# Latent attention of a two-layer kernel: four score banks, row maxima as single full-depth products, and no bank of their own for sums and outputs

## The chip, the cores and the metric

One core of one Trainium2 chip runs the whole program. The metric is the device time of one execution in microseconds, lower is better; the time of the kernel is the median of several executions.

## The reference, cut to what matters

The program is two transformer layers; the change lies in the first layer's attention alone. Per batch (B = 16) there are S = 100 queries in H = 16 heads and 1444 keys. The keys and the values are one and the same latent of 64 numbers, shared by all heads.

```
q_big = rope(einsum('bshk,hkq->bshq', (x @ Wq.T).reshape(B, S, H, K), w_kc_q))
kv_r  = rope(ctx)                                  # (B, 1444, 64)
q_r   = einsum('bshq,hqr->bhsr', q_big, W_qr)
k_r   = einsum('bld,hdr->bhlr', kv_r, W_kr)
attn  = softmax(einsum('bhsr,bhlr->bhsl', q_r, k_r), axis=-1)
ctx_c = einsum('bhsl,bld->bhsd', attn, kv_r)       # then w_kc_kv, Wo, + x
```

Before this stage the weights are folded, so that per batch there remains a query of 64 numbers for each of 1600 rows (head, position), which meets the 1444 latents directly. Queries and keys are held as a high part (fp32r) and the rest, for accuracy.

## The kernel before

**Stage and tiling.** `latent_attention` runs 16 batches in software pipeline. A batch has two halves p of eight heads and 12 tiles of 128 keys (`KT`), so `NS` = 24 values n = p * 12 + t; the program walks them in pairs, m = n // 2, from 0 to 11. Each n has two score tiles (o = 0, 1), 128 keys by 400 columns (four heads by 100 queries). Four score tiles belong to an m. Each engine has its order written out by hand in its own `step`, and semaphores (`at_...`) join the engines; nothing reorders them.

**A score tile.** `scores` (L814) makes it of two matmuls, KH x QS and KB x QB, into bank `S0 + (2n+o) % SB`, here three banks. KH holds the high part of the keys twice (rows 0 to 63 and 64 to 127), QS the high part of the queries and their rest, and the KB, QB pair the remaining product and the row maximum, which is subtracted inside the matmul. ScalarE (L780) takes the exponential into one of eight buffers of R. `values` (L824) multiplies R with KV, two n at a time and one m late, into bank CTX, in two halves of 64 columns of the array. VectorE (`sum_even`, L606 to L612) adds the tiles of o = 0 up in bank ACC, GpSimd (`sum_odd`, L628) those of o = 1 in EA.

**The row maxima.** The softmax maxima of batch b + 1 are found during batch b. `NF` = 39 products (13 tiles of 128 queries by 3 pieces of 482 keys) are made in 20 pairs: `max_pair` (L567) issues two matmuls of 64 rows, which use the upper and the lower half of the array at the same time, into banks F0 and F0 + 1, and one `reduce_pair` (L590) on VectorE reduces both banks to two columns of PM. Pair i waits for the reduction of pair i - 1. Two pairs stand in each of m = 0 to 9. `batch_max` (L596) then makes NM, `turn_max` (L573) transposes it, ScalarE and VectorE split it into MH and ML, and two DMAs bring these into QB, for which the next batch's first score waits.

**Sums and output.** `sums` (L637) reduces the accumulated exponentials over the partitions by a matmul with ones, for the earlier batch's second half at m = 2 (`SUM_AT`) and this batch's first half at m = 8 (`SUM0_AT`); `sums_out` on ScalarE copies them, a chain over `reciprocals` (L653, in n = 9) and DMAs leads to `divide` (L659, in n = 14), and `project` (L666) at m = 9 makes the earlier batch's output, which `add_output` adds. Sums, transpose and output share bank MISC. Banks: scores 0 to 2, maxima 3 and 4, CTX 5, ACC 6, MISC 7.

**Beside it.** GpSimd, ScalarE and VectorE also prepare the keys of batch b + 2 (`rotate_part`, `keys_high`); VectorE's part (L540, the lower part KB) comes at n = 18 and n = 20. The first batch has no earlier one beside it: its 20 pairs stand alone, in four banks, `max_pair` two deep. The last batch makes no maxima.

Of the kernel before, what the change touches and what calls it, by code (L numbers as in the profile page):

```python
# [20 lines left out]
P = 128  # L21
# [56 lines left out]
def as_f32(ap):  # L78

    return ap.bitcast(F32)  # L80
# [312 lines left out]
def latent_attention(core, dram, X, ident, queries, recips, BB):  # L393
# [25 lines left out]
    with ExitStack() as ctx:  # L419
# [127 lines left out]

        def f_bank(b, i):

            return S0 if b is FIRST and i % 2 else F0  # L550

        def pieces(i):
            return range(2 * i, min(2 * i + 2, NF))

        def max_pair(pe, b, i):

            r = b_mod(b)
            depth = 2 if b is FIRST else 1
            if i >= depth:
                pe.wait_ge(red_done, b_val(b) * NP + (i - depth + 1))  # L560
            elif b is not FIRST:
                pe.wait_ge(red_done, b_val(b) * NP)
            for f in pieces(i):
                t, j = divmod(f, KC)
                rows = slice((f % 2) * DC, (f % 2 + 1) * DC)
                high = QB if f % 2 else QS
                last = nc.tensor.matmul(psum[f_bank(b, i) + f % 2][:, 0:KW], high[r][rows, t * P:(t + 1) * P],  # L567
                                        KH[r][rows, KAT[j]:KAT[j] + KW], start=True, stop=True)
            last.then_inc(f_ready, 1)

        def turn_max(pe, b):
            pe.wait_ge(nm_ready, b_val(b) + 1)
            nc.tensor.transpose(psum[MISC][0:QT, 0:P], NM[:, :], ident[:, :]).then_inc(turned, 1)  # L573

        def max_high(act, b):
            act.wait_ge(turned, b_val(b) + 1)
            if b is not FIRST:
                act.wait_ge(m_in, b_val(b) * 32)
            nc.scalar.activation(MH[:, :], psum[MISC][0:QT, 0:P], ACT.Copy).then_inc(mh_ready, 1)

        def max_low(v, b):
            v.wait_ge(mh_ready, b_val(b) + 1)
            nc.vector.tensor_tensor(ML[:, :], psum[MISC][0:QT, 0:P], as_f32(MH[:, :]), ALU.subtract).then_inc(ml_ready, 1)

        def reduce_pair(v, b, i):
            v.wait_ge(f_ready, b_val(b) * NP + (i + 1))
            if i == 0 and b is not FIRST:
                v.wait_ge(nm_ready, b_val(b))
            k, n = f_bank(b, i), len(pieces(i))
            nc.vector.tensor_reduce(PM[:, 2 * i:2 * i + n], banks[:, k:k + n, 0:KW], AX.X, ALU.max).then_inc(red_done, 1)  # L590

        def batch_max(v, b):
            v.wait_ge(red_done, b_val(b) * NP + NP)
# [36 lines left out]
        def sums(pe, b, p):  # L630

            pe.wait_ge(even_sum, b_val(b) * NS + (EB + KT * (p + 1)))
            pe.wait_ge(odd_sum, b_val(b) * 2 * ADDS + ADDS * (p + 1))
            if p == 0 and b is not FIRST:
                pe.wait_ge(su_done, b_val(b) * 2)
            for o in range(2):
                last = nc.tensor.matmul(psum[MISC][o * DC:(o + 1) * DC, 0:CH], ones[:], ES[:, p, o, :], start=True, stop=True)  # L637
            last.then_inc(sum_done, 1)

        def sums_out(act, b, p):  # L640
            act.wait_ge(sum_done, b_val(b) * 2 + (p + 1))
            if b is not FIRST:
                act.wait_ge(sr_in, b_val(b) * 32)
            nc.scalar.activation(SU[:, p, :], psum[MISC][0:DC + 1, 0:CH], ACT.Copy).then_inc(su_done, 1)

# [16 lines left out]
        def project(pe, b):  # L662

            pe.wait_ge(ct_ready, b_val(b) + 2)
            for j in range(H // 2):
                last = nc.tensor.matmul(psum[MISC][0:S, 0:D], CT[:, j, :], BB[:, j, :], start=j == 0, stop=j == H // 2 - 1)  # L666
            last.then_inc(out_ready, 1)

        def add_output(v, b):
            v.wait_ge(out_ready, b_val(b) + 2)  # L670
            x = X[:, b_val(b), :]
            nc.vector.tensor_tensor(x, psum[MISC][0:S, 0:D], x, ALU.add).then_inc(res_done, 1)

# [11 lines left out]
        def b_mod(b):  # L685
            return b.r
# [14 lines left out]
        with nc.Block() as block:  # L701
# [50 lines left out]
            def _(act):  # L752
# [13 lines left out]
                def step(b, has_next, has_keys):  # L766
                    for n in range(NS):
                        if n == 2 * TURN_AT + 2 and has_next:
                            max_high(act, b + 1)
                        if n == 0 and b is not FIRST:  # L770
                            context_out(act, before(b), 1)
                        act.wait_ge(av_done, b_val(b) * NS + (n + 1))
                        act.wait_ge(even_sum, b_val(b) * NS + (n + 1))
# [7 lines left out]
                        if n in HI_AT and has_keys:  # L781
                            keys_high(act, b + 2, HI_AT.index(n))
                        if n == 2 * SUM_AT + 1 and b is not FIRST:
                            sums_out(act, before(b), 1)
                        if n == KT + 1:
                            context_out(act, b, 0)
                        if n == 2 * SUM0_AT + 1:
                            sums_out(act, b, 0)

# [5 lines left out]
            def _(pe):  # L795
# [5 lines left out]
                for i in range(NP):  # L801
                    max_pair(pe, FIRST, i)
                turn_max(pe, FIRST)
# [23 lines left out]

                def step(b, has_next, has_keys):
                    for m in range(NS // 2):
# [12 lines left out]
                        for n in (2 * m, 2 * m + 1):  # L842
                            scores(b, n)
                        if has_next and m and 2 * m + 1 < NP:
                            max_pair(pe, b + 1, 2 * m + 1)
                        if m == TURN_AT and has_next:
                            pe.wait_ge(su_done, b_val(b) * 2 + 1)
                            if b is not FIRST:
                                pe.wait_ge(res_done, b_val(b))
                            turn_max(pe, b + 1)  # L850
# [3 lines left out]
                        if m == SUM_AT and b is not FIRST:  # L854
                            sums(pe, before(b), 1)
                        if m == SUM0_AT:
                            sums(pe, b, 0)
                        if m == OUT_AT and b is not FIRST:
                            pe.wait_ge(su_done, b_val(b) * 2 + 1)
                            project(pe, before(b))  # L860

                steps(pe, step)
                for n in range(NS - 2, NS):
                    values(LAST, n)
                pe.wait_ge(res_done, B - 1)
                sums(pe, LAST, 1)
                pe.wait_ge(su_done, 2 * B)
                project(pe, LAST)

            @block.vector  # L870
            def _(v):
# [21 lines left out]
                for i in range(NP):  # L893
                    reduce_pair(v, FIRST, i)
                batch_max(v, FIRST)
# [4 lines left out]
                def step(b, has_next, has_keys):  # L900
                    for n in range(NS):
                        if has_next and n < NP:
                            reduce_pair(v, b + 1, n)
# [4 lines left out]
                        if has_next and n == NP - 1:  # L908
                            batch_max(v, b + 1)
# [4 lines left out]
                        if n == CT_AT and b is not FIRST:  # L914
                            divide(v, before(b))
                        if n == 2 * OUT_AT + 2 and b is not FIRST:
                            add_output(v, before(b))
                        if n == 2 * TURN_AT + 2 and has_next:
                            max_low(v, b + 1)

                steps(v, step)
# [1502 lines left out]
```

## Time and profile before

| | |
|---|---|
| median of 3 runs | 1990.33 us (1978.36 to 1990.39) |
| profiled execution, its own time | 1987.93 us |
| span of the profile | 1986.1 us |
| latent attention, first to last maximum product, then its tail | 309.7 to 1131, to 1207 us |
| TensorE matmul busy | 1710.8 us (86%) |
| VectorE, GpSimd, ScalarE busy | 1313.9, 902.8, 769.1 us |

The profile is one execution. PE is TensorE's matmuls and PEld its weight loads, which may overlap matmuls; DVE is VectorE, ACT ScalarE, POOL GpSimd, SP the engine that issues DMAs. A matmul's row lasts from its start to the modelled arrival of its last result, so neighbours overlap in time, and the time that each costs the stream is the distance from start to start. The rows below are read that way.

### The profile page before, as it was taken

The numbers are of one execution on the slowest core, as the hardware profiler recorded it, in microseconds if no ns is written. First come the engines' busy times: TensorE is split into PE (matmuls) and PEld (weight loads), VectorE is DVE, ScalarE is ACT, GpSimd is POOL, SyncE is SP. The second block draws the span as 40 slices with busy tenths as digits, with TensorE's granted clock in tenths as the row PEclk, the third lists the DMA queues.
The fourth block names the chain that finished last, engine by engine and source line by source line (L and its number), as shares of the span: only waits on it lengthen the run. The fifth ranks groups of instructions, "written<-read, shape, count | busy, mean of one in ns | idle before, by whom it ended". The sixth has DMA issues, their size and how long they took to land. (4 is left out here: it accounts for less than half of the span.)

```text
span 1986.1 us, 29082 instructions
## 1 busy us (share of the span) xinstructions
PE 1710.8 (86%) x9602; PEld 1155.4 (58%) x9602; DVE 1313.9 (66%) x2408; ACT 769.1 (39%) x1996; POOL 902.8 (45%) x800
## 2 busy tenths in 40 slices
PE   4999935999999999999999996499999559987890
PEld 3677712555555555555555553399999547664780
DVE  5577768777777777777777744377767666666333
ACT  2100001444444444444444442266656237652230
POOL 0366623777777777777777440223322100000436
PEclk9999965999999999999999996599999879988795
DMA  6133344122122221122221002545555250001243
GB/s 183 39 72 71 67 125 150 39 72 61 45 72 72 72 64 56 63 72 72 72 72 35 10 9 54 152 163 201 183 173 196 85 130 0 0 1 37 89 122 102
DMA packets 91670, 166.50 MB, mean 84 GB/s; under 512 B 45635, under 2 KB 70439, under 8 KB 86735
## 3 DMA queue, kind: packets, MB, share of 16 engines
q1 hardware_dynamic: 83727, 145.77, 23.8%
q0 software_dynamic: 7808, 19.02, 3.8%
q8 instruction: 73, 1.20, 0.3%
q14 instruction: 62, 0.51, 0.1%
HBM read 134.91 MB, written 29.53 MB: 83 GB/s over the span
## 5 line engine op out<-in xcount | busy, mean ns | idle before, releaser
L780 ACT ACTIVATE R<-banks 128x400 f32<-128x400 f32 x768 | 333.7, 505 | 342.4 <-PE banks L814 340.0
L590 DVE TENSOR_REDUCE PM<-banks 128x2 f32<-128x964 f32 x320 | 360.8, 1132 | 155.8 <-PE banks L567 154.1
L628 POOL TENSOR_TENSOR EA<-EA,R 128x400 f32<-128x400 f32 x288 | 313.3, 1088 | 177.8 <-ACT R L780 164.6
L814 PE MATMUL banks<-QS,KH 128*128 128x400 f32 x768 | 309.5, 403 | 3.0 <-DMA QB<-ML 2.1
L824 PE MATMUL banks<-R,KV 128*64 128x400 f32 x1536 | 299.9, 512 | 0.0
L814 PE MATMUL banks<-QB,KB 128*128 128x400 f32 x768 | 266.2, 347 | 0.0
L608 DVE TENSOR_TENSOR banks<-banks,R 128x400 f32<-128x400 f32 x320 | 183.9, 575 | 54.9 <-ACT R L780 54.2
L814 PEld LDWEIGHTS banks<-QS,KH 128*128 128x128 f32 x768 | 145.2, 189 | 109.0 <-ACT R L780 58.5
L567 PE MATMUL banks<-KH,QS 64*128 64x482 f32 x320 | 160.5, 502 | 53.5 <-DVE KB L540 46.3
L175 PE MATMUL banks<-e_xh,e_split 128*116 128x256 f32 x960 | 195.7, 287 | 4.0 <-DVE e_xl L1586 4.0
L380 POOL TENSOR_TENSOR rotated<-rope_prod 96x400 f32<-96x400 f32 x128 | 131.7, 1049 | 131.7 <-DVE rope_prod L357 131.6
L567 PEld LDWEIGHTS banks<-KH,QS 64*128 64x128 f32 x320 | 60.9, 191 | 197.2 <-issue 111.6
L824 PEld LDWEIGHTS banks<-R,KV 128*64 128x64 f32 x1536 | 93.4, 136 | 120.0 <-ACT R L780 67.1
L357 DVE TENSOR_TENSOR rope_prod<-banks,rope_q 96x400 f32<-96x400 f32 x256 | 128.6, 561 | 51.0 <-PE banks L175 51.0
L175 PEld LDWEIGHTS banks<-e_xh,e_split 128*116 128x116 f32 x960 | 153.1, 183 | 4.4 <-DVE e_xl L1586 4.4
L567 PE MATMUL banks<-KH,QB 64*128 64x482 f32 x304 | 153.0, 504 | 0.0
L814 PEld LDWEIGHTS banks<-QB,KB 128*128 128x128 f32 x768 | 146.5, 191 | 0.4
L1461 POOL DMA_INDIRECT results<-e_ys,m_target x40 | 44.4, 1109 | 213.1 <-DVE e_ys L1604 207.0
L175 PE MATMUL banks<-e_xl,e_split 128*116 128x256 f32 x480 | 136.7, 285 | 0.0
L521 POOL TENSOR_TENSOR raw<-raw,ropeT 128x722 f32<-128x722 f32 x60 | 104.0, 1735 | 53.8 <-DMA rawk<-in_ctx_k 53.8
L1052 POOL IOTA m_steps<- 100x7 f32 (+1 forms) x2 | 0.3, 158 | 237.8 <-POOLq L70 237.8
L1611 DVE TENSOR_TENSOR e_HF<-banks,e_G 116x256 f32<-116x256 f32 x120 | 50.5, 421 | 86.9 <-ACT e_G L1550 85.9
(281 smaller groups left out, 3368.9 us busy)
## 6 DMA issues: line engine op xcount, KB each, us to landing
m_stage_u<-in_m_up SPq DMA_DIRECT2D x20, 1392.0 KB
raw<-in_ctx_T SPq DMA_DIRECT2D x16, 1444.0 KB, 6.2
m_stage_d<-in_m_down SPq DMA_DIRECT2D x20, 696.0 KB
QS<-queries SPq DMA_DIRECT2D x16, 800.0 KB, 6.8
queries<-q_out_h SPq DMA_DIRECT2D x64, 100.0 KB, 2.4
queries<-q_out_l SPq DMA_DIRECT2D x64, 100.0 KB, 2.4
QB<-queries SPq DMA_DIRECT2D x16, 400.0 KB, 8.1
RS<-recips SPq DMA_DIRECT2D x32, 200.0 KB
```

Source lines behind the costliest of these rows:

```text
L175: ins = nc.tensor.matmul(out, lhs, rhs, start=first and n == 0, stop=last and n == len(todo) - 1)
L357: last = nc.vector.tensor_tensor(prod[:, h % 2, n, :].rearrange("p (b s) -> p b s", b=CB), psum[2 * (h % 2) + half][0:HALF, 0:CH].rearrang ...
L380: last = nc.gpsimd.tensor_tensor(rot[:, h % TURNS, half, :], prod[:, h % 2, 2 * half, :], prod[:, h % 2, 2 * half + 1, :], ALU.add)
L521: ins = ops.tensor_tensor(raw[:, row, half], raw[:, row, half], ropeT[:, row, half], ALU.mult)
L567: last = nc.tensor.matmul(psum[f_bank(b, i) + f % 2][:, 0:KW], high[r][rows, t * P:(t + 1) * P], KH[r][rows, KAT[j]:KAT[j] + KW], start=Tr ...
L590: nc.vector.tensor_reduce(PM[:, 2 * i:2 * i + n], banks[:, k:k + n, 0:KW], AX.X, ALU.max).then_inc(red_done, 1)
L608: ins = nc.vector.tensor_tensor(acc, acc, tile_of(n, 0), ALU.add)
L628: nc.gpsimd.tensor_tensor(out, first, tile_of(n, 1), ALU.add).then_inc(odd_sum, 1)
L780: nc.scalar.activation(tile_of(n, o), psum[S0 + (2 * n + o) % SB][:, 0:CH], ACT.Exp).then_inc(exp_done, 1)
L814: last = nc.tensor.matmul(out, lhs[r][:, keys], heads[:, o], start=lhs is KH, stop=lhs is KB)
L824: last = nc.tensor.matmul(psum[CTX][o * DC:(o + 1) * DC, 0:CH], KV[b_mod(b)][:, t, :], tile_of(n, o), start=t == 0, stop=t == KT - 1)
L1611: nc.vector.tensor_tensor(HF[:, b, :], psum[b][0:TR, TOK:2 * TOK], G[:, b, :], ALU.mult).then_inc(h_ready, 1)
```

## The change

- **Banks.** Scores get four banks (0 to 3, `SB` = 4), the maxima banks 4 and 5, CTX 6, ACC 7. MISC is gone: sums, transpose and its readers use the first bank of the maxima (F0), the output projection the second (F0 + 1).
- **Maxima.** `max_row` (L560 in the changed file) issues one product over all 128 rows, KH x QS, to bank F0 + f % 2, and waits for reduction f - 2; `reduce_row` (L610) reduces one bank. The table `MAX_AT` gives each m up to four slots: before the scores, between the two n, after them, and after the values. The first batch's maxima are still reduced in pairs (`first_max`, `first_reduce`), of full-depth products.
- **Guards.** Since banks are shared, `max_row` at f = 12 and f = 34 waits for ScalarE's copy of the sums, f = 0 and 1 for ML and the added output, `sums` for the reduction of the bank's last product.
- **Order.** The transpose now follows the values of m = 10, and the output projection moves from m = 9 to right behind it; `add_output` moves from n = 20 to n = 22; `batch_max` from n = 19 to n = 20.

```diff
-    SB, FB = 3, 2
+    SB = 4
-    S0, F0, CTX, ACC, MISC = 0, 3, 5, 6, 7
-    SUM_AT, SUM0_AT, OUT_AT, TURN_AT = 2, 8, 9, 10
+    S0, F0, CTX, ACC = 0, 4, 6, 7
+    SUM_AT, SUM0_AT, TURN_AT = 2, 8, 10
+    MAX_AT = ((1, 1, 1, 1),) * 3 + ((0, 1, 1, 1),) + ((1, 1, 1, 1),) * 4 + ((1, 1, 1, 0), (0, 1, 1, 1), (1, 1, 0, 0), (0, 0, 0, 0))
+    MAX_NO = [[sum(map(sum, MAX_AT[:m])) + sum(MAX_AT[m][:slot]) for slot in range(4)] for m in range(NS // 2)]
+    MAX_SUM, MAX_SUM0 = MAX_NO[SUM_AT + 1][0], MAX_NO[SUM0_AT + 1][0]
...
+        def max_product(b, f, bank):
+            t, j = divmod(f, KC)
+            return nc.tensor.matmul(psum[bank][:, 0:KW], QS[b_mod(b)][:, t * P:(t + 1) * P],
+                                    KH[b_mod(b)][:, KAT[j]:KAT[j] + KW], start=True, stop=True)
...
+        def max_row(pe, b, f):
+            if f == 0:
+                pe.wait_ge(ml_ready, b_val(b))
+            elif f == 1:
+                if b_val(b) >= 3:
+                    pe.wait_ge(res_done, b_val(b) - 2)
+            else:
+                pe.wait_ge(red_done, max_base(b) + (f - 1))
+            if f == MAX_SUM and b_val(b) >= 2:
+                pe.wait_ge(su_done, 2 * b_val(b) - 2)
+            if f == MAX_SUM0:
+                pe.wait_ge(su_done, 2 * b_val(b) - 1)
+            max_product(b, f, F0 + f % 2).then_inc(f_ready, 1)
...
+        def reduce_row(v, b, f):
+            v.wait_ge(f_ready, max_base(b) + (f + 1))
+            if f == 0:
                 v.wait_ge(nm_ready, b_val(b))
-            k, n = f_bank(b, i), len(pieces(i))
-            nc.vector.tensor_reduce(PM[:, 2 * i:2 * i + n], banks[:, k:k + n, 0:KW], AX.X, ALU.max).then_inc(red_done, 1)
+            nc.vector.tensor_reduce(PM[:, f:f + 1], psum[F0 + f % 2][:, 0:KW], AX.X, ALU.max).then_inc(red_done, 1)
...
                     for m in range(NS // 2):
...
-                        if has_next and 2 * m < NP:
-                            max_pair(pe, b + 1, 2 * m)
+                        max_slot(m, 0)
                         if m == 0:
                             if b is not FIRST:
                                 for n in range(NS - 2, NS):
                                     values(before(b), n)
-                            if has_next:
-                                max_pair(pe, b + 1, 1)
                             pe.wait_ge(m_in, b_val(b) * 32 + 32)
-                        for n in (2 * m, 2 * m + 1):
-                            scores(b, n)
-                        if has_next and m and 2 * m + 1 < NP:
-                            max_pair(pe, b + 1, 2 * m + 1)
-                        if m == TURN_AT and has_next:
...
+                        scores(b, 2 * m)
+                        max_slot(m, 1)
+                        scores(b, 2 * m + 1)
+                        max_slot(m, 2)
                         for n in (2 * m - 2, 2 * m - 1):
                             if n >= 0:
                                 values(b, n)
...
+                        max_slot(m, 3)
+                        if m == TURN_AT:
+                            if has_next:
+                                turn_max(pe, b + 1)
...
+                            if b is not FIRST:
+                                project(pe, before(b))
```

What this does to the order, at two places. In the names, KH0, QS0, QB0 and KB0 belong to the batch whose maxima are made, KH2, QS2, QB2 and KB2 to the batch whose scores are made. First TensorE at the end of m = 0 and the start of m = 1, before:

```order
L567 MATMUL banks<-KH0,QS0 128x482 [waits at_red]
L567 MATMUL banks<-KH0,QB0 128x482
L814 MATMUL banks<-QS2,KH2 128x400 [waits at_exp,at_min]
L814 MATMUL banks<-QB2,KB2 128x400
...
L814 MATMUL banks<-QS2,KH2 128x400 [waits at_exp]
L814 MATMUL banks<-QB2,KB2 128x400
L567 MATMUL banks<-KH0,QS0 128x482 [waits at_red]
L567 MATMUL banks<-KH0,QB0 128x482
L814 MATMUL banks<-QS2,KH2 128x400 [waits at_exp]
```

and in the changed kernel:

```order
L834 MATMUL banks<-QB2,KB2 128x400
L560 MATMUL banks<-KH0,QS0 128x482 [waits at_res]
L834 MATMUL banks<-QS2,KH2 128x400 [waits at_exp]
L834 MATMUL banks<-QB2,KB2 128x400
L834 MATMUL banks<-QS2,KH2 128x400 [waits at_exp]
L834 MATMUL banks<-QB2,KB2 128x400
L560 MATMUL banks<-KH0,QS0 128x482 [waits at_red] x3
L834 MATMUL banks<-QS2,KH2 128x400 [waits at_exp]
```

A pair stood after four score tiles; now product f = 1 stands after two of them, and f = 2, 3 and 4 stand in a row, each waiting for the reduction two places back. Second, VectorE in n = 18 and 19 (m = 9), before:

```order
L608 TENSOR_TENSOR banks<-banks,R 128x400 [waits at_evensum,at_exp]
L540 TENSOR_TENSOR KB0<-raw,KH0 64x722 [waits at_kh,at_rotstep]
L590 TENSOR_REDUCE PM<-banks 128x1 [waits at_f]
L608 TENSOR_TENSOR banks<-banks,R 128x400 [waits at_evensum,at_exp]
L596 TENSOR_REDUCE NM<-PM 128x13 [waits at_turned,at_red]
```

and in the changed kernel, from n = 18 to n = 20:

```order
L610 TENSOR_REDUCE PM<-banks 128x1 [waits at_f]
L544 TENSOR_TENSOR KB0<-raw,KH0 64x722 [waits at_kh,at_rotstep]
L610 TENSOR_REDUCE PM<-banks 128x1 [waits at_f]
L628 TENSOR_TENSOR banks<-banks,R 128x400 [waits at_evensum,at_exp]
L610 TENSOR_REDUCE PM<-banks 128x1 [waits at_f] x2
L628 TENSOR_TENSOR banks<-banks,R 128x400 [waits at_evensum,at_exp]
L610 TENSOR_REDUCE PM<-banks 128x1 [waits at_f]
L616 TENSOR_REDUCE NM<-PM 128x13 [waits at_turned,at_red]
```

Behind the first half of KB only one reduction was left; now four are, of the products f = 35 to 38.

## Rows read from the trace of the kernel before

**Rows 1.** Busy time of every engine in stretches (us, PE, PEld, DVE, ACT, POOL, then PEclk, DMA)

```profile
660.19:713.80 53.61, 53.61 (x260) 28.80 (x258) 39.78 (x51) 24.25 (x55) 39.17 (x33) 1.00 0.21 67
...
300.00:330.00 30.00, 14.40 (x39) 5.57 (x39) 28.87 (x31) 1.50 (x2) 12.27 (x9) 0.50 0.46 145
```

**Rows 2.** Timeline of PE, one m: start us, length us, engine, line, operation

```profile
681.85 0.48 PE L567 MATMUL banks<-KH,QS 64*128 64x482 f32 x1
...
682.27 0.45 PE L814 MATMUL banks<-QS,KH 128*128 128x400 f32 x1
682.56 0.34 PE L814 MATMUL banks<-QB,KB 128*128 128x400 f32 x1
...
683.29 0.34 PE L814 MATMUL banks<-QB,KB 128*128 128x400 f32 x1
683.58 0.46 PE L814 MATMUL banks<-QS,KH 128*128 128x400 f32 x1
683.88 0.34 PE L814 MATMUL banks<-QB,KB 128*128 128x400 f32 x1
684.15 0.48 PE L567 MATMUL banks<-KH,QS 64*128 64x482 f32 x1
...
684.57 1.56 PE L824 MATMUL banks<-R,KV 128*64 128x400 f32 x8
686.06 0.48 PE L567 MATMUL banks<-KH,QS 64*128 64x482 f32 x1
```

**Rows 3.** Timeline of PE, scores straight after values

```profile
656.83 0.45 PE L814 MATMUL banks<-QS,KH 128*128 128x400 f32 x1
657.12 0.34 PE L814 MATMUL banks<-QB,KB 128*128 128x400 f32 x1
```

**Rows 4.** PE weight loads: timeline, then the list of waits for 350 to 1200 us

```profile
683.58 0.19 PEld L814 LDWEIGHTS banks<-QS,KH 128*128 128x128 f32 x1 [0.28 <-ACT R L780]
...
PEld banks L814 <- ACT R L780: 56.7, 202, 0.6
```

**Rows 5.** Timeline of ACT

```profile
683.02 1.74 ACT L780 ACTIVATE R<-banks 128x400 f32<-128x400 f32 x4 [2.47 <-PE banks L814]
```

**Rows 6.** Groups by form (count, busy us, mean ns); line 540 (ns min/median/max)

```profile
L590 DVE TENSOR_REDUCE PM<-banks 128x2 f32<-128x964 f32 x304 | 350.3, 1157 | 154.8 <-PE banks L567 153.5
...
L590 DVE TENSOR_REDUCE PM<-banks 128x1 f32<-128x482 f32 x16 | 10.5, 658 | 1.1 <-PE banks L567 0.6
...
L540 DVE TENSOR_TENSOR KB<-raw,KH x32: 903/909/1745, 307.8 to 1080.7; 64x722 fp32r<-64x722 f32 x32
```

**Rows 7.** Timelines of DVE (the last row: of POOL)

```profile
681.55 0.57 DVE L608 TENSOR_TENSOR banks<-banks,R 128x400 f32<-128x400 f32 x1
682.03 0.75 DVE L653 RECIPROCAL RR<-SR 16x100 f32<-16x100 f32 x1
...
684.68 1.16 DVE L590 TENSOR_REDUCE PM<-banks 128x2 f32<-128x964 f32 x1 [0.39 <-PE banks L567]
...
692.35 0.98 DVE L659 TENSOR_TENSOR CT<-CU,RS 128x800 f32<-128x800 f32 x1
...
701.55 1.75 DVE L540 TENSOR_TENSOR KB<-raw,KH 64x722 fp32r<-64x722 f32 x1
703.32 0.66 DVE L590 TENSOR_REDUCE PM<-banks 128x1 f32<-128x482 f32 x1
704.01 0.58 DVE L608 TENSOR_TENSOR banks<-banks,R 128x400 f32<-128x400 f32 x1
...
1131.39 0.66 DVE L590 TENSOR_REDUCE PM<-banks 128x1 f32<-128x482 f32 x1 [0.62 <-PE banks L567]
1131.96 0.57 DVE L608 TENSOR_TENSOR banks<-banks,R 128x400 f32<-128x400 f32 x1
...
701.48 1.04 POOL L628 TENSOR_TENSOR EA<-EA,R 128x400 f32<-128x400 f32 x1 [2.11 <-ACT R L780]
```

**Rows 8.** The first batch: timeline of DVE

```profile
310.47 20.96 DVE L590 TENSOR_REDUCE PM<-banks 128x2 f32<-128x964 f32 x20 [0.95 <-PE banks L567]
```

More of the change, by code:

```diff
@@ L411, in latent_attention @@
     PAD = -1.0e30
-    S0, F0, CTX, ACC, MISC = 0, 3, 5, 6, 7
-    SUM_AT, SUM0_AT, OUT_AT, TURN_AT = 2, 8, 9, 10
+    S0, F0, CTX, ACC = 0, 4, 6, 7
[3 more added lines that the diff above has]
+    MAX_SUM, MAX_SUM0 = MAX_NO[SUM_AT + 1][0], MAX_NO[SUM0_AT + 1][0]
+    assert sum(map(sum, MAX_AT)) == NF and MAX_SUM % 2 == 0 and MAX_SUM0 % 2 == 0
     RECIP_AT, CT_AT = 9, 14
@@ L546, in keys_high, with max_base @@
             nc.scalar.activation(KH[b_mod(b)][:, half], raw[:, 0, half], ACT.Copy).then_inc(kh_ready, 1)
-        def f_bank(b, i):
-            return S0 if b is FIRST and i % 2 else F0
+        def max_base(b):
+            return NP + (b_val(b) - 1) * NF if b is not FIRST else 0
         def pieces(i):
             return range(2 * i, min(2 * i + 2, NF))
[L555 to L562, printed above, removed]
-            for f in pieces(i):
[L564 to L568, printed above, removed]
-            last.then_inc(f_ready, 1)
+        def max_product(b, f, bank):
+            t, j = divmod(f, KC)
+            return nc.tensor.matmul(psum[bank][:, 0:KW], QS[b_mod(b)][:, t * P:(t + 1) * P],
+                                    KH[b_mod(b)][:, KAT[j]:KAT[j] + KW], start=True, stop=True)
@@ L636, in sums @@
             for o in range(2):
-                last = nc.tensor.matmul(psum[MISC][o * DC:(o + 1) * DC, 0:CH], ones[:], ES[:, p, o, :], start=True, stop=True)
+                last = nc.tensor.matmul(psum[F0][o * DC:(o + 1) * DC, 0:CH], ones[:], ES[:, p, o, :], start=True, stop=True)
             last.then_inc(sum_done, 1)
@@ L665, in project @@
             for j in range(H // 2):
-                last = nc.tensor.matmul(psum[MISC][0:S, 0:D], CT[:, j, :], BB[:, j, :], start=j == 0, stop=j == H // 2 - 1)
+                last = nc.tensor.matmul(psum[F0 + 1][0:S, 0:D], CT[:, j, :], BB[:, j, :], start=j == 0, stop=j == H // 2 - 1)
             last.then_inc(out_ready, 1)
@@ L771, in step @@
                             context_out(act, before(b), 1)
+                        if n == 2 * SUM_AT + 2 and b is not FIRST:
+                            sums_out(act, before(b), 1)
+                        if n == 2 * SUM0_AT + 2:
+                            sums_out(act, b, 0)
                         act.wait_ge(av_done, b_val(b) * NS + (n + 1))
@@ L801, in _ @@
                 for i in range(NP):
-                    max_pair(pe, FIRST, i)
+                    first_max(pe, i)
                 turn_max(pe, FIRST)
@@ L828, in step, with max_slot @@
                 def step(b, has_next, has_keys):
+                    def max_slot(m, slot):
+                        if has_next and MAX_AT[m][slot]:
+                            max_row(pe, b + 1, MAX_NO[m][slot])
                     for m in range(NS // 2):
@@ L854, in step @@
                         if m == SUM_AT and b is not FIRST:
+                            if has_next:
+                                pe.wait_ge(red_done, max_base(b + 1) + (MAX_SUM - 1))
+                            else:
+                                pe.wait_ge(ml_ready, b_val(b) + 1)
                             sums(pe, before(b), 1)
                         if m == SUM0_AT:
+                            if has_next:
+                                pe.wait_ge(red_done, max_base(b + 1) + (MAX_SUM0 - 1))
                             sums(pe, b, 0)
-                        if m == OUT_AT and b is not FIRST:
-                            pe.wait_ge(su_done, b_val(b) * 2 + 1)
-                            project(pe, before(b))
+                        max_slot(m, 3)
+                        if m == TURN_AT:
+                            if has_next:
+                                turn_max(pe, b + 1)
+                            elif b is not FIRST:
+                                pe.wait_ge(res_done, b_val(b) - 1)
+                            if b is not FIRST:
+                                project(pe, before(b))
                 steps(pe, step)
@@ L915, in step @@
                             divide(v, before(b))
-                        if n == 2 * OUT_AT + 2 and b is not FIRST:
-                            add_output(v, before(b))
                         if n == 2 * TURN_AT + 2 and has_next:
                             max_low(v, b + 1)
+                        if n == 2 * TURN_AT + 2 and b is not FIRST:
+                            add_output(v, before(b))
                 steps(v, step)
```

46 lines of the change are left out of this document (23 added, 23 removed).

## The prediction

> **What bounds the kernel now.** I went from the coarse view to the fine one. The window over one whole batch of the latent attention [rows 1] shows TensorE busy for all of 53.61 us at the full clock (1.00, 2.4 GHz), VectorE for 39.78, ScalarE for 24.25, GpSimd for 39.17. So TensorE's own stream is the batch: a term counts only if it lengthens or shortens that stream. "Busy" hides small losses, though, because a matmul's row lasts longer than its turn. I therefore read start to start [rows 2], over m = 5: a pair of 64-row maximum products 0.42 us (681.85 to 682.27), eight score products 1.88 (to 684.15), a second pair 0.42, the values 1.49 (684.57 to 686.06). That is 4.21 us, and it repeats. Inside the 1.88 the normal step is 0.183 us (four from 682.56 to 683.29), but the first takes 0.29 (0.11 more; the same after values [rows 3]), the last, ahead of 64-row products, 0.27 (0.10 more, counting both roundings), and the two from 683.29 to 683.88 take 0.59. There the weight load stood until 683.58 for an exponential [rows 4]: ScalarE began the first of that m at 683.02 and needs 0.5 us (four take 1.74 in steps of 0.41) [rows 5]. With three score banks the fourth tile needs the bank of the first. The list of waits counts 202 such waits, once for nearly each of the 16 x 12 values of m.
>
> **What the fourth bank removes.** Eight normal steps are 1.46; with the 0.11 and the 0.10 they make 1.67, and 0.21 us of the 1.88 are the wait. With four banks a tile needs the exponential four tiles back, which by then has had about 2.5 us of maxima and values to finish in. ScalarE has four at about 0.41 us each per 4.2 us, so nothing takes this wait's place there. I take all of it: 12 x 0.21 = **-2.5 us per batch**.
>
> **The maximum products.** Before: 19 pairs at 0.415 and one single at 0.41, 8.3 us. After: 39 products of the full depth, 482 columns. No row shows one. Its nearest row is the score product, 400 columns in 0.183 us; in proportion it is 0.22, and 482 columns at 2.4 GHz are 0.20. I take 0.217, 8.5 us: **+0.2 us** (bounds -0.5 and +0.3). They have the scores' tile shape, so between scores they need no extra 0.11. The blocks between values stay 12 (the lone product between the two blocks of values at m = 0 costs 0.21, the merged maxima of m = 0 and 1 save 0.21), and scores at m = 10 are now followed by values instead of the transpose: **+0.1**. Sums, transpose and output projection change place but not length; ScalarE's copies of the sums keep their place between exponentials, and the chain recips, RS, divide had no wait at its divide in a middle batch. The transpose now comes after values and before the projection, so its 3.35 us still lie ahead of the next batch's scores, as cover for the max row's DMAs.
>
> **The reductions.** One reduction of 964 elements took 1.157 us, one of 482 took 0.658 [rows 6]; 39 of these are 25.7 us against 22.6, so VectorE gets 3.1 us more per batch, 43 of 53.6. As a sum that is hidden: an m then costs it four steps of 0.57 (1131.39 to 1131.96) and two even sums of 0.48 (681.55 to 682.03) [rows 7], 3.25 us of about 4.0. What binds is latency: two banks now serve as a ring of single products, and product f waits for reduction f-2. Before, a pair waited for a reduction that had 1.9 us or more.
>
> **The new waits, worked out.** A pair's reduction starts 0.53 us after its first product (684.15 to 684.68) [rows 2, 7], 0.05 after the product's row of 0.48 ends. A full product in the stream has a row of about 0.38 (a score's 0.34, 82 columns more), so its reduction starts 0.43 after it; the first in a block, 0.54. Then 0.658, and 0.05 for the signal (exponential's end at 683.53, load at 683.58) [rows 4, 5]. A full product that was held pays 0.11 for its uncovered load. (a) f = 2, 3, 4 stand in a row, since m = 0 has no values of its own batch: f = 4 would follow f = 2 by two steps of 0.22 and the 0.08 that f = 3 waits, 0.51 us, but may start its work only 0.43 + 0.66 + 0.05 + 0.11 = 1.25 after it: 0.73. f = 3 and 5 lose 0.08 and 0.11, by the same steps. (b) In the usual m the second product has, from the product behind the values, 0.33 + 0.22 + 0.73 = 1.28 of cover, and needs 0.54 + 0.66 + 0.05 + 0.11 = 1.36: 0.08, five times, 0.4. (c) The reciprocal (0.75) [rows 7] now comes ahead of the reduction of the next m's first product: 0.3. (d) The divide (0.98) in m = 7: 0.15. (e) In m = 9 the half of KB (701.55, 1.75 us) stands between the reductions of f = 34 and 35: f = 37 may start at 0.43 + 0.58 + 1.77 + 0.66 + 0.05 + 0.11 = 3.60 after f = 34, and the stream brings it at 3.09: 0.5, and f = 38 another 0.1. Together **+2.4 us per batch** at 14 or 15 batches. (e) depends on GpSimd: the 1.75 us row began while GpSimd was busy from 701.48 [rows 7], while the middle one of the 32 such operations took 0.91 [rows 6]. The Trainium skill (SBUF — State Buffer, Who interferes with whom) says that a VectorE operation with two SBUF inputs and a GpSimd one that reads SBUF exclude each other by a lock; this trace agrees, 1.75 us against 0.91. If by shifted timing the lock is missed, (e) goes, 0.5 us per batch or 8 in all; I keep it, since the GpSimd sum stands at the same tile in both kernels.
>
> **Outside the steady batches.** The last batch has no maxima and keeps its whole gain, -2.5. In the first batch's 39 products, the clock is at 1.2 GHz (0.50 in [rows 1]) and VectorE's reductions set the pace: twenty in 20.96 us, the last a single, 1.07 each [rows 8]. Serial full products take 0.40 each there instead of two at once: signal 0.05, load 0.17, first 0.40, second to its reduction 0.66, and 1.16 of reduction make 2.44 per two pairs against 2.14: 0.15 x 19 = +2.8, if the clock stays at 1.2; 0 if it rises.
>
> **Sum.** 15 x (-2.5 + 0.2 + 0.1 + 2.4) = 15 x 0.2 = +3.0; -2.5; +2.8: +3 us on the profiled execution's 1987.93, which is 1991. The three runs' median is 1990.33, 2.4 above it, so **1991 us** stands for the median as well. The wait for the exponential is replaced by one for the reductions of nearly the same size.
>
> **Rivals.** (1) *The ring holds less than I count.* If reductions start sooner after a product (0.35) and follow one another at 0.50, the waits fall to about 1.2 us per batch: 15 x (-2.2 + 1.2) - 2.5 + 2.8 = -15, 1973. With no waits it is 15 x -2.2 + 0.3 = -33: 1955. For it: VectorE is idle 14 us of a batch. Against: (a) and (e) follow from the order alone. (2) *VectorE's pace is worse, slower.* The one single reduction in a middle batch held VectorE for 0.69 (703.32 to 704.01) [rows 7], not 0.57. At 0.69 an m costs 3.7 us, and (b) to (e) grow from 1.5 to 2.6: 15 x 1.2 + 0.3 = +18, 2006; if each reduction also starts 0.54 after its product and not 0.43, +2.0 per batch, 2018. It decides from +1.3 us per batch on, a pace of about 0.7. [...] Against: the row follows the KB operation, and 1131.39 without it has 0.57. (3) *The fourth bank does nothing*, because the wait at 683.58 is for something else that stays: then 15 x 2.7 + 2.8 = +43: 2031. Against: it ends 0.05 after the exponential's end.
>
> **How the numbers follow.** Forecast (within 12 us of 1991) 0.60; (1) 0.21; (2) 0.16; (3) 0.03. The ends of the forecast are -0.5 and +0.3 on the products, 0.5 on (e), 3 at the start. The range reaches halfway into (1) and over most of (2): 1966 to 2011. A measurement tells 1%, 20 us, from no change: faster (under 1970) is most of (1), 0.16; slower (over 2010) is the worse part of (2) and (3), 0.12; same 0.72.
>
> **What would show it.** In the profile after: the score tiles' load waits on ScalarE gone, eight scores and four products in a row 0.18 and 0.22 apart; weight loads of the maximum products waiting on the reductions, the longest at f = 4 and f = 37, with a sum near 2.4 us per batch (36 in all); a batch of 53.6 to 53.9 us; reductions near 0.66. I am wrong if the full products step above 0.25, if the waits on reductions sum to under 1.4 or over 3.5 us per batch, or if the exponentials still hold scores.

## The result, and the profile after

The changed kernel takes **2009.93 us** (median of 4 runs, 2004.01 to 2015.11) against 1988.63 for the kernel before (4 runs): ratio 1.0124, interval 1.0086 to 1.0161. It is slower by 1.2%; the forecast was no change, 1991 us. The profiled execution took 2004.01 us, 16.1 more than the 1987.93 of before; it is the shortest of the four.

The page's first lines and the costliest groups of the changed kernel (engine, busy us, share, count; then line, busy us, mean ns, idle before) answer to [rows 6]:

```profile
PE 1702.0 (85%) x9602; PEld 1217.0 (61%) x9602; DVE 1338.0 (67%) x2693; ACT 780.5 (39%) x1996; POOL 908.4 (45%) x800
...
L610 DVE TENSOR_REDUCE PM<-banks 128x1 f32<-128x482 f32 x585 | 365.0, 650 | 161.7 <-PE banks L560 161.1
...
L560 PE MATMUL banks<-KH,QS 128*128 128x482 f32 x624 | 262.1, 452 | 71.7 <-DVE KB L544 46.2
```

TensorE is busy for 9 us less in a span 16 us longer: the loss is idle time. The list of waits from 350 to 1220 us says on whom (us, times, longest) and answers to [rows 4]:

```profile
PEld banks L560 <- DVE PM L610: 58.5, 118, 3.4
...
PEld banks L834 <- DMA QB<-ML: 8.5, 6, 3.6
...
PEld banks L834 <- ACT R L804: 0.6, 1, 0.6
```

The waits of scores on ScalarE are gone but for one of 0.6 us; they were 56.7 us in 202 before. Those on reductions were to be 36 us, the longest under 1 us; they are 58.5, the longest 3.4.

**Where in time.** A fixed landmark is the reciprocal, once per batch. From the first to the 14th of these there are 697.4 us before (413.94 to 1111.30, twelve periods of 53.61 to 53.63 and a last one of 53.91) and 716.4 after (415.75 to 1132.11): +19.0. Of 13 periods after, eight are 54.06 to 54.15; the others are 55.79, 56.81, 58.25, 58.25 and 54.41. So 13 x 0.47 = 6 us are lost evenly and 13 us in five batches. At the first reciprocal the changed kernel is 1.8 us late, and from the 14th to the last it gives back 3.5. One ordinary batch in windows (columns as in [rows 1]), whose first row there it answers to; the second answers to the other, and the third follows it:

```profile
757.00:811.10 54.10, 53.02 (x257) 32.51 (x256) 40.90 (x71) 25.05 (x55) 39.72 (x33) 1.00 0.21 67
300.00:330.00 30.00, 17.25 (x32) 8.15 (x32) 26.99 (x29) 1.50 (x2) 10.82 (x8) 0.50 0.47 145
340.00:350.00 10.00, 9.54 (x37) 6.87 (x36) 6.43 (x12) 4.77 (x9) 4.15 (x4) 0.80 0.90 310
```

**The ring's waits are as forecast.** PE's timeline at the three products in a row (f = 2 to 5; scores of L834 between), then at f = 37:

```profile
671.28 0.35 PE L834 MATMUL banks<-QB,KB 128*128 128x400 f32 x1
671.47 0.35 PE L834 MATMUL banks<-QS,KH 128*128 128x400 f32 x1
671.65 0.35 PE L834 MATMUL banks<-QB,KB 128*128 128x400 f32 x1
671.84 0.65 PE L560 MATMUL banks<-KH,QS 128*128 128x482 f32 x2
672.98 0.49 PE L560 MATMUL banks<-KH,QS 128*128 128x482 f32 x1 [0.49 <-DVE PM L610]
673.30 0.35 PE L834 MATMUL banks<-QS,KH 128*128 128x400 f32 x1
...
657.01 0.49 PE L560 MATMUL banks<-KH,QS 128*128 128x482 f32 x1
657.72 0.48 PE L560 MATMUL banks<-KH,QS 128*128 128x482 f32 x1 [0.21 <-DVE PM L610]
```

f = 4 starts 1.14 us after f = 2, where two free steps are 0.44: 0.70 lost, forecast 0.81 (0.73 and the 0.08 of f = 3). At 657.72 the step is 0.71 and not 0.22: 0.5, forecast 0.5. Scores step 0.185, undisturbed by exponentials.

**The divide is not.** Its line, as minimum, median and maximum ns, in the changed kernel:

```profile
L679 DVE TENSOR_TENSOR CT<-CU,RS x16: 991/1634/4380, 425.8 to 1216.4; 128x800 f32<-128x800 f32 x16
```

In [rows 7] it took 0.98 us. Two batches of the changed kernel, VectorE and GpSimd, the ordinary case first:

```profile
646.01 0.65 DVE L610 TENSOR_REDUCE PM<-banks 128x1 f32<-128x482 f32 x1
646.58 1.65 DVE L679 TENSOR_TENSOR CT<-CU,RS 128x800 f32<-128x800 f32 x1
...
646.35 1.03 POOL L648 TENSOR_TENSOR EA<-EA,R 128x400 f32<-128x400 f32 x1
647.35 2.57 POOL L539 TENSOR_TENSOR KV<-rawk,prodk 128x768 f32<-128x768 f32 x1
...
700.70 4.34 DVE L679 TENSOR_TENSOR CT<-CU,RS 128x800 f32<-128x800 f32 x1
704.97 0.65 DVE L610 TENSOR_REDUCE PM<-banks 128x1 f32<-128x482 f32 x1
...
700.39 1.05 POOL L648 TENSOR_TENSOR EA<-EA,R 128x400 f32<-128x400 f32 x1
701.39 1.83 POOL L539 TENSOR_TENSOR KV<-rawk,prodk 128x768 f32<-128x768 f32 x1
703.16 1.04 POOL L648 TENSOR_TENSOR EA<-EA,R 128x400 f32<-128x400 f32 x1
```

GpSimd begins a running sum 0.2 to 0.3 us ahead of the divide. In the ordinary case the divide ends 0.85 after that sum's end (647.38), and KV, next on GpSimd, is the one that is stretched: 2.57 against 1.83. At 700.70 KV and the following sum keep their usual length, and the divide ends 0.84 after the end of the *third* GpSimd operation. In the kernel before the divide came first in each of the first 14 batches:

```profile
692.40 1.82 POOL L628 TENSOR_TENSOR EA<-EA,R 128x400 f32<-128x400 f32 x1 [0.18 <-ACT R L780]
```

GpSimd had waited for an exponential there, and the divide of 692.35 slipped in 0.05 us ahead of it; the sum took 1.82 instead of 1.04, which nobody waited for. So the two operations exclude each other. The Trainium skill (SBUF — State Buffer, Who interferes with whom) says the same of VectorE operations with two SBUF inputs and GpSimd operations that read SBUF: an exclusive lock on a shared port pair. By that rule, the trace agrees.

What TensorE made of the 4.34 us (timeline of weight loads, then windows in the columns of [rows 1]):

```profile
705.67 0.19 PEld L560 LDWEIGHTS banks<-KH,QS 128*128 128x128 f32 x1 [3.40 <-DVE PM L610]
```

```profile
702.50:705.50 3.00, 0.07 (x1) 0.00 (x0) 3.00 (x2) 0.00 (x0) 1.70 (x2) 1.00 0.00 0
705.50:710.00 4.50, 4.33 (x15) 3.58 (x17) 3.24 (x7) 2.16 (x5) 1.10 (x2) 0.62 0.00 0
710.00:714.00 4.00, 4.00 (x24) 2.40 (x22) 2.37 (x5) 2.60 (x6) 1.55 (x2) 1.00 0.01 2
```

The maximum product's load stood for 3.4 us behind the reduction queued after the divide. TensorE had done nothing for 3.1 us, and the granted clock fell from 2.4 to 1.2 GHz for a stretch: 0.62 as the mean of the second window, scores 0.33 us apart until about 709, and 1.00 again from 710. In the batch of 589.77, whose load stood just as long (594.73), the loads that follow still take 0.19 us, so the clock had not fallen, and its period is 2.7 us too long, not 4.1: 2.7 is the stall, 1.4 the clock. Three divides of 4.34 to 4.38 cost 11.0 of the 13 uneven us. Most of the rest, 1.7 us of one period, is a load at 505.01 that waited 2.37 us for ML:

```profile
505.01 0.19 PEld L834 LDWEIGHTS banks<-QS,KH 128*128 128x128 f32 x1 [2.37 <-DMA QB<-ML]
```

### The profile page after: what moved, and what is told of

It is laid out like the page before. It is cut to its first block and busy times, and to the rows that moved or that the text cites. A ratio compares the mean times of both kernels' runs of the same rounds, so it can differ in the third digit from the quotient of the medians.

```text
span 2002.2 us, 29381 instructions
## 1 busy us (share of the span) xinstructions
PE 1702.0 (85%) x9602; PEld 1217.0 (61%) x9602; DVE 1338.0 (67%) x2693; ACT 780.5 (39%) x1996; POOL 908.4 (45%) x800
## 5 line engine op out<-in xcount | busy, mean ns | idle before, releaser
L804 ACT ACTIVATE R<-banks 128x400 f32<-128x400 f32 x768 | 342.8, 503 | 346.3 <-PE banks L834 328.6
L610 DVE TENSOR_REDUCE PM<-banks 128x1 f32<-128x482 f32 x585 | 365.0, 650 | 161.7 <-PE banks L560 161.1
L560 PE MATMUL banks<-KH,QS 128*128 128x482 f32 x624 | 262.1, 452 | 71.7 <-DVE KB L544 46.2
L834 PE MATMUL banks<-QS,KH 128*128 128x400 f32 x768 | 275.1, 358 | 4.6 <-DMA QB<-ML 4.6
L834 PE MATMUL banks<-QB,KB 128*128 128x400 f32 x768 | 267.5, 348 | 0.0
L560 PEld LDWEIGHTS banks<-KH,QS 128*128 128x128 f32 x624 | 115.0, 197 | 207.6 <-issue 119.5
L834 PEld LDWEIGHTS banks<-QS,KH 128*128 128x128 f32 x768 | 146.5, 191 | 32.8 <-issue 20.0
L834 PEld LDWEIGHTS banks<-QB,KB 128*128 128x128 f32 x768 | 146.4, 191 | 9.8
L2209 ACT ACTIVATE c_PR<-banks,c_nmax 100x100 f32<-100x100 f32 x256 | 84.2, 356 | 49.6 <-DVE c_nmax L2253 49.6
```

What stands on the lines that cost most here:

```text
L560: return nc.tensor.matmul(psum[bank][:, 0:KW], QS[b_mod(b)][:, t * P:(t + 1) * P], KH[b_mod(b)][:, KAT[j]:KAT[j] + KW], start=True, stop=True)
L610: nc.vector.tensor_reduce(PM[:, f:f + 1], psum[F0 + f % 2][:, 0:KW], AX.X, ALU.max).then_inc(red_done, 1)
L804: nc.scalar.activation(tile_of(n, o), psum[S0 + (2 * n + o) % SB][:, 0:CH], ACT.Exp).then_inc(exp_done, 1)
L834: last = nc.tensor.matmul(out, lhs[r][:, keys], heads[:, o], start=lhs is KH, stop=lhs is KB)
L2209: nc.scalar.activation(PR[u][:, h, :], psum[SC + 2 * u + h // HB][0:S, (h % HB) * S:(h % HB + 1) * S], ACT.Exp, bias=nmax[u][:, 1, h:h + 1 ...
```

## The experiments

Times are medians; "before" is the kernel before on the same chip. A batch is the usual period in steady state, 53.62 before and 54.10 in the changed kernel.

**e1_div_late**: the divide two tiles later, n = 16.

```diff
-    RECIP_AT, CT_AT = 9, 14
+    RECIP_AT, CT_AT = 9, 16
```

> The changed kernel with one number changed: the divide of the earlier batch stands on VectorE in n = 16 and not in n = 14, behind GpSimd's last key-preparation step. Theory A (GpSimd keeps VectorE's divide from starting, 1.6 us in most batches and 4.3 in three of the profile's, 3.4 us of TensorE's stream each plus a stretch at the lower clock): every divide takes 0.98 us, no weight load waits over 1 us for a reduction in mid batch, and the time falls by 10 to 20 us against the changed kernel's 2010, to 1990 to 2000. Theory B (the loss is in the ring of two banks alone, the long divides are a symptom): the time stays within 5 us of 2010.

Measured: 1980.12 against 1985.81, ratio 0.9961 (0.9946 to 0.9977); batch 53.43. One number turns a loss of 1.2% into a gain of 0.4%; the time is 10 us below the expected 1990 to 2000. The divide and the waits on reductions:

```profile
L679 DVE TENSOR_TENSOR CT<-CU,RS x16: 993/1478/1773, 428.1 to 1193.9; 128x800 f32<-128x800 f32 x16
```

```profile
PEld banks L560 <- DVE PM L610: 37.9, 88, 0.8
```

The expected 0.98 did not come: the divide still takes 1.48 us, for GpSimd is busy there too, but never more than 1.8. m = 8 leaves out a product, so little waits for it: where it took 1.77 and not 1.49, the period was 53.48 and not 53.43. The ring with what is left of the divide now waits 37.9 us; the forecast was 36.

**e2_before_div12**: in the kernel before, the divide at n = 12, where GpSimd goes from one operation to the next.

```diff
-    RECIP_AT, CT_AT = 9, 14
+    RECIP_AT, CT_AT = 9, 12
```

> The kernel before with one number changed: the divide stands in n = 12 and not in n = 14, where GpSimd has instructions back to back (668.7 to 692.2 us in the profile of before) and not a pause. Theory A (lock-out by GpSimd, whatever the maxima look like): the divide takes 2 to 4.5 us in most batches, TensorE waits for the pair reductions behind it, and the kernel is slower by 15 to 45 us, 2005 to 2035. Theory B (the long divides belong to the changed kernel's ring): the divide stays at 0.98 us and the time at 1990.

Measured: 2004.85 against 1985.81, 1.0100 (1.0083 to 1.0117); batch 54.84. That is just under the expected 2005 to 2035, and one divide of the 13 took over 2 us, not most of them. One batch:

```profile
697.28 1.98 DVE L659 TENSOR_TENSOR CT<-CU,RS 128x800 f32<-128x800 f32 x1
...
696.68 1.74 POOL L532 TENSOR_TENSOR raw<-raw 128x722 f32<-128x722 f32 x1
698.37 1.79 POOL L628 TENSOR_TENSOR EA<-R 128x400 f32<-128x400 f32 x1
...
700.40 0.18 PEld L567 LDWEIGHTS banks<-KH,QS 64*128 64x128 f32 x1 [1.85 <-DVE PM L590]
```

Nothing of 4 us appears (maximum 2.16): the divide never waited for more than one GpSimd operation, and in every batch it ended 0.85 us after that one.

```profile
643.43 1.00 DVE L659 TENSOR_TENSOR CT<-CU,RS 128x800 f32<-128x800 f32 x1 [1.13 <-DMA RS<-recips]
```

The run is not clean, though. At n = 12 the divide also comes too early for the DMA of RS. Over the 13 batches VectorE stood idle 7 us for that DMA, and the divides were 8 us longer than 0.98 in all; where RS came latest (643.43) the divide took 1.00, and the period was 54.84 as elsewhere. So e2 shows that the exclusion also strikes in the old structure, with its paired reductions, and not that it alone costs 1% there.

**e3_sb3**: the changed kernel with three score banks.

```diff
-    SB = 4
+    SB = 3
```

> The changed kernel with three score banks in use and not four (the fourth serves only the first batch's maxima). My forecast's term: the wait for the exponential comes back, 0.21 us in each of 12 m of 16 batches, less where a wait for a reduction already covers it: slower than the changed kernel by 25 to 40 us, 2035 to 2050. Rival (the fourth bank does nothing): 2010.

Measured: 2027.02 against 1985.81, 1.0200 (1.0180 to 1.0221). Neither 2035 to 2050 nor 2010 came. Beside the changed kernel's 2009.93 it looks as if the bank were worth 17 us, but the profile (2040.25, the longest of the five executions) has eight divides of 4.31 to 4.66 us where the changed kernel's has three, and an ordinary batch is 54.27, only 0.17 more. The time says nothing on the bank; that takes a run without the lock-outs (e10).

**e4_short_reduce**: the reductions read 241 of the 482 columns. This leaves half of the keys out of the maxima.

```diff
-            nc.vector.tensor_reduce(PM[:, f:f + 1], psum[F0 + f % 2][:, 0:KW], AX.X, ALU.max).then_inc(red_done, 1)
+            nc.vector.tensor_reduce(PM[:, f:f + 1], psum[F0 + f % 2][:, 0:KW // 2], AX.X, ALU.max).then_inc(red_done, 1)
```

> The changed kernel in which each single reduction reads 241 of its 482 columns (it leaves out half of the keys' maxima), 0.41 us in place of 0.66. If the ring of two banks costs what I worked out, the waits of about 2.4 us per batch fall to about 0.9, since every one of them holds one reduction's length or more: 15 x 1.5 = 22 us, and VectorE's spare time rises by 9 us a batch. Divides locked out remain, with less behind them. 1975 to 1990. If the ring costs little, within 8 us of 2010.

Measured: 1967.14 against 1985.81, 0.9906 (0.9882 to 0.9929), single runs 1956.33 to 1986.35; batch 51.75. A batch is 2.35 us shorter, and the time is 8 us below what was expected: latency of reductions is what TensorE pays for, though 0.67 of the 2.35 is the divide's (e12). The wide spread probably goes with the divide: in this profile two take 5.57 us, behind four GpSimd operations in a row, and the four runs of e12 lie within 4.1 us.

**e9_before_div16**: control, the kernel before with the divide at n = 16 (diff as in e1).

> Control: the kernel before with the divide in n = 16, the same edit that took 30 us off the changed kernel. In the kernel before, the divide of n = 14 already took 0.98 us, in a pause of GpSimd, so there is nothing to win: within 5 us of the kernel before (about 1986). If it gains 10 us or more, the edit has another effect than the one I name, and the 30 us are not all lock-out.

Measured: 1984.30 against 1987.90, 0.9991 (0.9972 to 1.0010); divide 0.98, batch 53.61. The move alone brings nothing; what e1 won is the repair of a loss that the change had made.

**e10_sb3_div16**: the changed kernel with `CT_AT` = 16 and `SB` = 3.

> The changed kernel with the divide in n = 16 and three score banks. The run with three banks and the divide in n = 14 had a batch of 54.3 us against 54.1 with four, so my theory is that the fourth bank is worth 0.2 us a batch: 3 to 5 us slower than the run with four banks and the divide in n = 16 (1980), 1983 to 1986. The maximum product between the second and the third score tile gives ScalarE the 0.2 us that the fourth tile used to wait. My forecast's term (2.5 us a batch from the bank itself) would give 2018.

Measured: 1981.57 against 1987.90, 0.9968 (0.9951 to 0.9986); batch 53.60 against 53.43 in e1. In a batch with maxima the fourth bank is worth **0.17 us**; the times of e10 and e1 lie within each other's intervals. The wait of [rows 4] is nearly gone without it:

```profile
PEld banks L834 <- ACT R L804: 7.8, 28, 0.3
...
711.58 0.19 PEld L834 LDWEIGHTS banks<-QS,KH 128*128 128x128 f32 x1 [0.28 <-ACT R L804]
```

Where the 28 stand tells why. In a batch with maxima it is one (in one batch two), at m = 11 (the row), the one m that has no maximum product between its score pairs. In the last batch, without maxima, it is again one for nearly each m (12 from 1142 us on), and there the bank is worth what was forecast, 2.5: the stretches from the 14th to the 15th and to the 16th reciprocal take 46.07 and 34.39 us with three banks, 45.04 and 32.74 with four (e1), together 2.7 less.

**e7_all**: the changed kernel, divide at n = 16, and three moves against what remained: at m = 0 the earlier batch's values stand behind slot 2, hence between the products f = 2 and f = 3 (ScalarE's copy of the context one tile later for it), and SP issues MH and ML ahead of the keys.

```diff
-    RECIP_AT, CT_AT = 9, 14
+    RECIP_AT, CT_AT = 9, 16
...
+                    if has_next:
+                        max_rows(sp, b_val(b + 1), b_mod(b + 1))
...
-                        if n == 0 and b is not FIRST:
+                        if n == 1 and b is not FIRST:
...
+                        if m == 0 and b is not FIRST:
+                            for n in range(NS - 2, NS):
+                                values(before(b), n)
```

> The changed kernel with three moves: the divide in n = 16; the earlier batch's last two value blocks of m = 0 behind that m's scores and third maximum product (and ScalarE's copy of the context one n later), so that the products f = 2, 3 and 4 no longer stand in a row; and on the DMA queue the two rows of maxima ahead of the next keys' loads. The ring costs 0.8 to 0.9 us a batch at f = 3, 4 and 5 (0.70 at f = 4 in the trace): 15 x 0.85 = 13 us below the run with the divide in n = 16 (1980), and the waits for the DMA of the maxima, 3 us outside the first batch, go too: 1962 to 1970. If those waits only reappear at the next product, within 4 us of 1980.

Measured: 1968.76 against 1987.90, 0.9912 (0.9892 to 0.9932); batch 52.63, 0.80 under e1. (a) was forecast at 0.92 in all. The waits on ML, 8.5 us in 6 in the changed kernel and 8.2 in 7 in e1, fell to one of 1.2.

**e8_keys_late**: e7, and the halves of KB at n = 20 and 21 instead of 18 and 20, behind the reductions.

```diff
-    HI_AT, LO_AT = (17, 18), (18, 20)
+    HI_AT, LO_AT = (17, 18), (20, 21)
```

> The run before (three moves) and a fourth: VectorE's two operations for the low part of the keys in n = 20 and 21 and not in n = 18 and 20, behind the last reduction. The waits at f = 37 and 38, 0.6 us a batch by the trace, go: 15 x 0.6 = 9 us below the three moves, 1953 to 1961. If the keys now come late for the loads of the next keys or the next batch, slower than the three moves.

Measured: 1955.81 against 1987.90, **0.9840** (0.9820 to 0.9859): faster than both kernels. One batch in the columns of [rows 1], and its waits on reductions from 400 to 1180 us:

```profile
684.18:736.18 52.00, 52.00 (x258) 32.57 (x257) 40.52 (x71) 24.82 (x55) 39.20 (x33) 1.00 0.23 67
```

```profile
PEld banks L560 <- DVE PM L610: 12.9, 28, 0.6
```

A batch is 0.63 shorter than in e7; (e) was forecast at 0.6. In this view TensorE is busy through all of 52.00 us again, as it was in the kernel before.

**e11_kv_late**: the changed kernel, divide left at n = 14, and GpSimd's KV operation moved from n = 14 to 16.

```diff
-    ROT_AT = (3, 4, 5, 6, 8, 9, 10, 11, 13, 14)
+    ROT_AT = (3, 4, 5, 6, 8, 9, 10, 11, 13, 16)
```

> The lock from the other side: the changed kernel with the divide left in n = 14 and GpSimd's last preparation step (KV, 1.83 us) moved from n = 14 to n = 16. In the three bad batches the divide stood behind three GpSimd instructions back to back, the sum of n = 14, KV and the sum of n = 15. Without KV there, GpSimd has to wait for ScalarE between its sums and the divide gets in: no divide over 2 us, no stretch at the lower clock in mid attention; the 0.6 us per batch of the ordinary divides may stay. 1990 to 2000 against 2010. If the length of the divide has another cause, the bad batches stay and the time is 2005 to 2015.

Measured: 1990.16 against 1989.96, 1.0002 (0.9982 to 1.0022); batch 54.10 as in the changed kernel. The divide:

```profile
698.29 1.60 DVE L679 TENSOR_TENSOR CT<-CU,RS 128x800 f32<-128x800 f32 x1
...
698.00 2.77 POOL L648 TENSOR_TENSOR EA<-EA,R 128x400 f32<-128x400 f32 x2
```

No divide is over 1.9 us, in a profile that is the longest of the ten executions. Moving GpSimd's operation and nothing on VectorE removes all long lock-outs, and the median falls by 20 us; the even 0.47 per batch stays. This separates the two costs.

**e12_short_div16**: e4's edit and e1's. Half of the keys are left out of the maxima, as in e4.

> The short reductions (241 of 482 columns, half of the maxima left out) with the divide in n = 16, so that the ring is sized alone, against the run with the divide in n = 16 and full reductions (1980, a batch of 53.4 us). By my sum of the waits, 2.4 us a batch, each holds one reduction, which is 0.25 us shorter: the waits at f = 4, 37, 38, 21, 5 and the small ones fall by 0.1 to 0.25 each, 1.5 in all: a batch of 51.9, 1957 to 1962. If the ring costs nothing, 1980.

Measured: 1952.16 against 1989.96, 0.9824 (0.9793 to 0.9856); batch 51.75, 1.68 under e1 where no long lock-out disturbs either; 1.5 was expected, and 1957 to 1962. That is what 241 columns less per reduction are worth; 18.4 us of waits on reductions, in 28, are left.

## Why the prediction was wrong, point by point

**The step that failed is term (d)**, "The divide (0.98) in m = 7: 0.15". Its duration was taken from the row of 692.35 in [rows 7] as if it belonged to the instruction. It belonged to the place: there GpSimd had a pause, and the divide was 0.05 us ahead of it. The changed order puts VectorE 0.2 to 0.3 us *behind* GpSimd's sum and nearer to the next product. The prediction had named this exclusion for KB in (e), in the same paragraph, and not asked the question for the other large operation. In place of 0.15 the runs show

- 0.67 us in every ordinary batch (54.10 against 53.43 in e1), where the divide is 0.65 us longer than the 0.98 assumed, in an m with four slots. That its length is what costs there, the one odd batch shows: at 871.34 it took 1.93, 0.30 more than its neighbours, and the period was 54.41, 0.29 more. A divide of 0.98 in that place was not run;
- 2.7 us, or 4.1 where the clock fell, in batches where GpSimd kept its turn for three operations: 11.0 us in the profile.

The profiled execution was to be 3 us longer and was 16.1: the lock-outs 11.0; the ordinary divide (0.67 - 0.15) x 13 = 6.8; the wait for ML 1.7; against that the ring 0.24 x 13 = 3.1 cheaper, start and last batch 1.0 each, and a rest of 1.3. The other executions ran 5 to 11 us longer still; that these had more lock-outs is not shown by a trace, but e11, whose profile has none, is at 1.0002 where the changed kernel is at 1.0124.

**The ring, (a), (b), (c), (e) = 2.2: right.** The steady batch with the divide out of the way is 53.43 (e1), by the forecast without (d) 53.67; the waits sum to 37.9 us, forecast 36; (a) is 0.80 of 0.92 (e7) and (e) 0.63 of 0.6 (e8).

**The products, +0.2, and the reductions: right.** Full products step 0.22, reductions take 0.65 and step 0.57 (704.97 is followed by a sum at 705.54). Rival (2), a worse pace of VectorE, had the right sign and the wrong mechanism: the pace did not change, one operation was locked out.

**The fourth bank, -2.5: right as a sum, wrong as a cause in the batches with maxima.** The waits on exponentials did vanish. But with three banks they nearly vanish as well (e10): the maximum product that now stands between two score pairs, 0.22 us long, gives ScalarE the 0.21 us that [rows 4] showed missing. Where no such product stands, at m = 11 and in the last batch, the wait is there with three banks and gone with four. Rival (3) held that the bank does nothing and the wait stays; for these batches the first half is nearly true. That the sum came out all the same is luck: both parts were in the change, and the expectation of e3, which rested on the bank alone, failed.

**Outside the steady batches.** The 1.8 us at the first reciprocal are not the first batch's twin products. The first product already starts 1.5 us later (309.66 before, 311.17 in the changed kernel), ahead of anything that was changed, and e1, the same up to that reciprocal, reaches it at 413.94 like the kernel before. Within the stage:

```profile
331.47 0.20 DVE L596 TENSOR_REDUCE NM<-PM 128x13 f32<-128x39 f32 x1
...
337.12 0.77 PE L567 MATMUL banks<-KH,QS 64*128 64x482 f32 x1 [1.26 <-DVE PM L590]
...
337.82 0.70 PE L814 MATMUL banks<-QS,KH 128*128 128x400 f32 x1
```

```profile
335.95 0.20 DVE L616 TENSOR_REDUCE NM<-PM 128x13 f32<-128x39 f32 x1
...
339.48 0.77 PE L560 MATMUL banks<-KH,QS 128*128 128x482 f32 x1 [2.89 <-DVE KB L544]
...
340.22 0.70 PE L834 MATMUL banks<-QS,KH 128*128 128x400 f32 x1
```

From the first product to NM there are 21.8 us before and 24.8 after: +3.0, forecast +2.8, at the clock of 0.50 that was assumed; it rose only behind the first score (340 to 350 us: 0.80). What the forecast left out follows: a second pair stood ahead of the first score and waited for the reduction of the one before it. Now one product stands there, and from it to the score there are 0.74 us and not 2.73 (335.09 to 337.82). So only 0.9 is left at the first score and 0.3 at the first reciprocal.

The last batch gave 3.5, forecast 2.5; 2.7 of it is the fourth bank (e10). What was not forecast is ML: SP issued its DMA late, right behind the keys' 1.8 MB, at 722.43 with the keys at 719.91 and 720.29, against 657.22 with 652.63 and 653.02 before; issued ahead of them (e7), all but one of the waits went. "Cover for the max row's DMAs" counted the time from the transpose and not what lies ahead of them in the queues.

**What is open.** With the same distance between sum and divide (0.31 us) the divide got its turn after one GpSimd operation in some batches and after three in others; with three banks it was after three in eight batches of 13. No run tells what decides, so the number of such batches can't be forecast. All that were seen had operations back to back on GpSimd; in e11, with a pause after the sum, none came.

## What to carry to other kernels

The duration of the divide, a VectorE operation with two SBUF inputs, was here a property of its place and not of its shape: before moving such an operation, or anything that shifts it by some tenths of a us, look at what GpSimd has queued there, and price it from free to the whole row of GpSimd's operations. When a wait disappears in a change of several parts, test the part that is given the credit alone, here by one number, and only after the disturbances are out: e3 put the bank at 17 us, e10 at 0.17 per batch with maxima. The same holds for a control: e2 moved the divide into the lock and into a wait for a DMA at once. And the ring two deep was paid in latency: products spaced by other work, and long operations moved behind the last reduction, were worth 1.4 us per batch at unchanged work.

## What was unexpected of the hardware

- A 0.98 us VectorE operation took 4.34 us behind three GpSimd operations (of 1.05, 1.83 and 1.04) and 5.57 behind four. The turn does not go to the waiting side at each boundary.
- The exclusion costs the one that comes second: 0.05 us ahead of GpSimd the divide took 0.98 and GpSimd's sum 1.82; 0.2 to 0.3 behind it 1.6, with the next GpSimd operation at 2.57 instead of 1.83.
- A weight load held for 3.4 us, with TensorE idle for 3.1, was followed by the lower clock twice and once not, which decides between a loss of 2.7 and of 4.1 us. In e3 the lower clock came in all eight such batches.
